# Gram products for two samples at a time in every tile, with two turning banks instead of four

## The reference

```python
e = jnp.stack([tbl_0[ids[:, 0]], ..., tbl_31[ids[:, 31]]], axis=1)
dots = jnp.einsum('bnd,bmd->bnm', e, e)
z = dots[:, iu, ju]                       # 496 pairs i < j
h = jnp.concatenate([z, dense_ctx], axis=1)
h = jnp.maximum(h @ W_top1 + b_top1, 0.0) # 512 -> 512
h = jnp.maximum(h @ W_top2 + b_top2, 0.0) # 512 -> 256
y = h @ W_top3                            # 256 -> 1
```

## Time and profile before

| | |
|---|---|
| median of 3 runs | 896.95 us (895.36 to 898.39) |
| profiled execution, its own time | 892.55 us |
| its span, first to last instruction | 890.7 us |
| TensorE matmuls | 601.0 us busy, 67%, 11019 matmuls |
| TensorE weight loads | 524.1 us, 59% |
| VectorE | 225.9 us, 25% |
| ScalarE | 204.6 us, 23% |
| GpSimd | 398.0 us, 45% |
| mean granted TensorE clock | 0.85 |

### The profile page before, as it was taken

How to read it: one execution, slowest core, us unless ns; L and a number is a source line. 1 busy time by engine, 2 the same in 40 slices (tenths; PEclk the granted TensorE clock), 3 DMA queues, 4 the chain that set the end, 5 groups by cost and what they waited for, 6 DMA issues and landing times.

```text
span 890.7 us, 24184 instructions
## 1 busy us (share of the span) xinstructions
PE 601.0 (67%) x11019; PEld 524.1 (59%) x11019; DVE 225.9 (25%) x578; ACT 204.6 (23%) x369; POOL 398.0 (45%) x426
## 2 busy tenths in 40 slices
PE   3557668486684867748577584875848668486687
PEld 2456557375572756737467474765737657375586
DVE  3444313123130231402223032231312313123122
ACT  4252303103030030401313022130210303103042
POOL 7563625526255361543715347262462625526220
PEclk9688969698796987969789697896969969698799
DMA  9962312313122141321313224131231312313110
GB/s 220 243 204 68 99 42 77 94 44 102 43 78 83 50 107 38 83 73 56 108 37 87 63 57 118 32 96 49 70 105 39 101 41 76 88 41 90 43 38 2
DMA packets 37459, 70.97 MB, mean 80 GB/s; under 512 B 10382, under 2 KB 23438, under 8 KB 37358
## 3 DMA queue, kind: packets, MB, share of 16 engines
q0 software_dynamic: 20112, 54.95, 22.1%
q1 hardware_dynamic: 17246, 14.48, 7.0%
HBM read 69.39 MB, written 0.01 MB: 78 GB/s over the span
## 4 chain that ended last, share of the span: by engine, by line
PE 42%; another core or an unknown queue 30%; issue 13%; ACT 12%; DMA 1%; DVE 1%; POOL 1%; ACTq 0%; DVEq 0%
PE look_ps L338 18%; PE quad_ps L358 12%; PE top_ps L420 6%; ACT turned L501 4%; ACT turned L483 3%; PE turn_ps L322 3%; PE quad_ps L322 2%; ACT area L550 2%; ACT ahead L490 1%; DMA rows<-in_tbl,row_ids 1%; PE quad_ps L377 1%; POOL rows L295 1%; PE top_ps L407 1%; ACT products L506 0%
## 5 line engine op out<-in xcount | busy, mean ns | idle before, releaser
L295 POOL DMA_INDIRECT rows<-in_tbl,row_ids x419 | 397.2, 948 | 458.1 <-PE turn_ps L322 184.1
L338 PE MATMUL look_ps<-one_hot,small 125*128 125x256 f32 (+1 forms) x1536 | 251.9, 303 | 104.7 <-issue 92.8
L338 PEld LDWEIGHTS look_ps<-one_hot,small 125*128 125x128 f32 x1536 | 214.0, 202 | 116.6 <-issue 112.3
L358 PE MATMUL quad_ps<-turned 128*32 128x31 f32 x7680 | 140.0, 204 | 121.8 <-issue 121.5
L358 PEld LDWEIGHTS quad_ps<-turned 128*32 128x32 f32 x7680 | 108.8, 115 | 166.9 <-issue 153.3
L674 DVE TENSOR_SCALAR one_hot<-ids_across,sub_row 125x256 fp32r<-125x256 int32 (+1 forms) x384 | 112.0, 364 | 145.8 <-PE look_ps L338 126.6
L322 PE MATMUL turn_ps<-ident,rows 128*128 128x128 f32 x424 | 64.5, 282 | 28.5 <-issue 14.7
L655 DVE TENSOR_TENSOR top_ps<-top_ps,b_sb 128x256 f32<-128x256 f32 x15 | 6.5, 433 | 299.8 <-PE top_ps L420 299.8
L490 ACT ACTIVATE ahead<-look_ps 128x512 f32<-128x512 f32 (+1 forms) x48 | 28.3, 590 | 232.5 <-PE look_ps L338 219.1
L407 PE MATMUL top_ps<-area,w_sb 128*128 128x128 f32 x488 | 61.9, 276 | 19.5 <-issue 18.8
L550 ACT ACTIVATE area<-top_ps,b_sb 128x128 f32<-128x128 f32 x61 | 17.5, 368 | 227.5 <-remote 225.2
(11 more groups left out here) (50 smaller groups left out, 169.9 us busy)
## 6 DMA issues: line engine op xcount, KB each, us to landing
rows<-in_tbl,row_ids POOLq DMA_INDIRECT x419
ids_across<-in_small_ids SPq DMA_DIRECT2D x45, 128.0 KB
landed<-in_tbl SPq DMA_DIRECT2D x6, 896.0 KB
w_sb<-in_W_top SPq DMA_DIRECT2D x4, 256.0 KB
landed<-in_tbl SPq DMA_DIRECT2D x6, 104.0 KB
w_sb<-in_W_top SPq DMA_DIRECT2D x1, 512.0 KB
area<-in_dense_ctx SPq DMA_DIRECT2D x16, 8.0 KB
row_ids<-in_ids SPq DMA_DIRECT2D x1, 240.0 KB
```

The lines of the kernel that those rows point to most:

```text
L295: pool.indirect_dma_start(out=rows[:, n % PLACES, j, :], out_offset=None, in_=tables[f], in_offset=bass.IndirectOffsetOnAxis(ap=row_ids[:, ...
L338: last = pe.matmul(look_ps[:, c * width:(c + 1) * width], small[:, f, r, part, c * P:(c + 1) * P], one_hot[n % 2][:, r, 0:width], start=(r ...
L358: last = pe.matmul(gram_ps[q * FIELDS:(q + 1) * FIELDS, g // BANK_GROUPS, at:at + COLS], turned[:, c, s, :], turned[:, c, s, 0:COLS], star ...
```

## The change

The scheme of the last tile is used in all tiles. `last_gram`, `last_unfold` and their semaphores go; `gram`, `unfold` and `align` take their place. The results take four banks of their own, so turning has two (`RING = 2`). Two units instead of four are turned early, after portions 5 and 6, and ScalarE's units are the even ones. ScalarE aligns banks 0 and 2, VectorE banks 1 and 3, in every tile. The ids of each tile are laid out on the host as those of the last tile were, so that neighbouring samples stand side by side.

```diff
-    ACT_UNITS = [0, 1, 2, 6, 8, 10, 12]
-    RING = 4
+    ACT_UNITS = [0, 2, 4, 6, 8, 10, 12]
+    RING = 2
-    EARLY_AFTER = [3, 4, 5, 6]
+    EARLY_AFTER = [5, 6]
-    BANK_GROUPS = GROUPS // 2
+    GRAM_BANKS = 4
+    BANK_GROUPS = GROUPS // GRAM_BANKS
-        quad_ps = psum("quad_ps", [P, LAST_BANKS, 512])
-        gram_ps = quad_ps[:, 0:2, :]
-        turn_ps = [psum(f"turn_ps{i}", [P, 512]) for i in range(RING - 2)] + [quad_ps[:, b, :] for b in (2, 3)]
+        gram_ps = psum("gram_ps", [P, GRAM_BANKS, 512])
+        turn_ps = [psum(f"turn_ps{i}", [P, 512]) for i in range(RING)]
...
                 for g in range(portion * GPP, (portion + 1) * GPP):
-                    at = g % BANK_GROUPS * COLS
-                    for c in range(CHUNKS):
-                        for q in range(QUADS):
-                            s = q * FIELDS + g
-                            last = pe.matmul(gram_ps[q * FIELDS:(q + 1) * FIELDS, g // BANK_GROUPS, at:at + COLS],
-                                             turned[:, c, s, :], turned[:, c, s, 0:COLS],
-                                             start=(c == 0), stop=(c == CHUNKS - 1))
-                if portion == PARTS - 1:
-                    last.then_inc(gram_done, 1)
+                    at = g % BANK_GROUPS * WIDE
                     for c in range(CHUNKS):
                         for h in range(HALVES):
                             s = QUADS * g + 2 * h
                             pair = turned[:, c, s:s + 2, :]
+                            last = pe.matmul(gram_ps[h * 2 * FIELDS:(h + 1) * 2 * FIELDS, g // BANK_GROUPS, at:at + WIDE],
+                                             pair.rearrange("d s f -> d (s f)"), pair[:, :, 0:COLS],
+                                             start=(c == 0), stop=(c == CHUNKS - 1))
+                if (portion + 1) * GPP % BANK_GROUPS == 0:
+                    last.then_inc(gram_banks, 1)
...
-                    for i in ACT_UNITS[:3]:
+                    for i in ACT_UNITS[:2]:
                         keep_turned(BEGIN[t] + i)
                     if FIRST[t] > FIRST[t - 1]:
                         keep_looked_up(FIRST[t] - 1)
+                    keep_turned(BEGIN[t] + ACT_UNITS[2])
                     pick(t - 1)
...
+                align(t, 0)
                 for n in range(FIRST[t], FIRST[t + 1] - 1):
                     keep_looked_up(n)
-            align(0)
-            align(2)
+                align(t, 2)
...
             def unfold(t):
-                dve.wait_ge(gram_done, t + 1)
+                dve.wait_ge(act_aligned, 4 * (t + 1))
+                dve.wait_ge(dve_aligned, 4 * (t + 1))
...
                 for k, n in enumerate(range(FIRST[t] + 1, FIRST[t + 1] + 1)):
+                    if n == FIRST[t + 1]:
+                        align(t, 1)
                     if n < len(LOOKUPS):
                         make_one_hot(n)
...
-            align(1)
-            align(3)
-            last_unfold()
+                    align(t, 1)
+                align(t, 3)
+            unfold(TILES - 1)
...
-    by_slot[-P:] = by_slot[-P:].reshape(P // FIELDS, FIELDS, -1).transpose(1, 0, 2).reshape(P, -1)
+    by_slot = by_slot.reshape(TILES, P // FIELDS, FIELDS, -1).transpose(0, 2, 1, 3).reshape(BATCH, -1)
```

More of the change, by code:

```diff
@@ L81, in dlrm_tower @@
     GPP = GROUPS // PARTS
-    BANK_GROUPS = GROUPS // 2
     HALVES = 2
     WIDE = 2 * COLS
-    LAST_BANKS = 4
-    LAST_GROUPS = GROUPS // LAST_BANKS
+    GRAM_BANKS = 4
+    BANK_GROUPS = GROUPS // GRAM_BANKS
     AT_ONCE = 2
@@ L157, in dlrm_tower @@
         last_h1 = [top_ps, look_ps, turn_ps[0], turn_ps[1]]
-        last_h2 = turn_ps[2]
+        last_h2 = gram_ps[:, 0, :]
         spare_ps = turn_ps[0]
@@ L166, in dlrm_tower @@
         high_ps = [bank[0:SP, 0:AT_ONCE * D].rearrange("p (r d) -> p r d", r=AT_ONCE)
-                   for bank in (gram_ps[:, 1, :], top_ps)]
+                   for bank in (gram_ps[:, GRAM_BANKS - 1, :], top_ps)]
         square = products[:, 0:COLS * ZROW].rearrange("p (i j) -> p i j", j=ZROW)
@@ L191, in dlrm_tower @@
         dve_kept = sem("dve_kept")
-        gram_done = sem("gram_done")
-        last_gram_done = sem("last_gram_done")
+        gram_banks = sem("gram_banks")
         act_aligned = sem("act_aligned")
@@ L350, in gram @@
                         pe.wait_ge(unfolded, t)
-                if t == 0 and portion == PARTS // 2:
+                if t == 0 and portion * GPP == GROUPS - BANK_GROUPS:
                     pe.wait_ge(low_parts, SMALL * STEPS)
                 for g in range(portion * GPP, (portion + 1) * GPP):
-                    at = g % BANK_GROUPS * COLS
-                    for c in range(CHUNKS):
-                        for q in range(QUADS):
-                            s = q * FIELDS + g
-                            last = pe.matmul(gram_ps[q * FIELDS:(q + 1) * FIELDS, g // BANK_GROUPS, at:at + COLS],
-                                             turned[:, c, s, :], turned[:, c, s, 0:COLS],
-                                             start=(c == 0), stop=(c == CHUNKS - 1))
-                if portion == PARTS - 1:
-                    last.then_inc(gram_done, 1)
[L364 to L372, removed]
+                    at = g % BANK_GROUPS * WIDE
                     for c in range(CHUNKS):
@@ L456, in _ @@
                     look_between(t, k)
[L457 to L460, removed]
+                    gram(t, k)
                     if t > 0 and k == 0:
@@ L480, in keep_turned @@
                 if t > 0:
-                    act.wait_ge(gram_done, t)
+                    act.wait_ge(gram_banks, GRAM_BANKS * t)
                 f = unit[0]
@@ L514, in pick, with align @@
                 act.activation(features[:, CYCLIC:PAIRS], diagonal[:, 0:HALF, HALF], ACT.Copy).then_inc(picked, 1)
-            def align(b):
-                act.wait_ge(last_gram_done, b + 1)
-                both = quad_ps[:, b, 0:LAST_GROUPS * WIDE].rearrange("p (g h j) -> p h g j", h=2, j=COLS)
+            def align(t, b):
+                act.wait_ge(gram_banks, GRAM_BANKS * t + b + 1)
+                both = gram_ps[:, b, 0:BANK_GROUPS * WIDE].rearrange("p (g h j) -> p h g j", h=2, j=COLS)
                 for q in (1, 3):
@@ L606, in keep_turned @@
                 if t > 0:
-                    dve.wait_ge(gram_done, t)
+                    dve.wait_ge(gram_banks, GRAM_BANKS * t)
                 f = unit[0]
@@ L613, in unfold, with align @@
             def unfold(t):
-                dve.wait_ge(gram_done, t + 1)
+                dve.wait_ge(act_aligned, 4 * (t + 1))
+                dve.wait_ge(dve_aligned, 4 * (t + 1))
                 if t > 0:
                     dve.wait_ge(picked, t * PICKS)
[L617 to L623, removed]
+                grams = gram_ps[:, :, 0:BANK_GROUPS * WIDE].rearrange("p b (g h j) -> p h j b g", h=2, j=COLS)
+                dve.transpose(square[:, 0:COLS, 0:FIELDS], grams[:, 0, :, :, :]).then_inc(unfolded, 1)
+            def align(t, b):
+                dve.wait_ge(gram_banks, GRAM_BANKS * t + b + 1)
+                both = gram_ps[:, b, 0:BANK_GROUPS * WIDE].rearrange("p (g h j) -> p h g j", h=2, j=COLS)
                 for q in (1, 3):
@@ L626, in align @@
                     dve.tensor_copy(both[at, 0, :, :], both[at, 1, :, :]).then_inc(dve_aligned, 1)
[L628 to L633, removed]
             def last_pick():
```

## The result

The changed kernel takes 945.76 us (median of 4 runs, 942.7 to 947.63), the kernel before beside it 896.15 us (4 runs, 894.34 to 898.39): 1.0549 times as long, with an interval of 1.0506 to 1.0592. Forecast were 927 us, and 885 to 960 as the range. The profiled execution's own time is 943.9 us, its span 942.1. Medians are of all executions of a kernel and ratios of its fast ones alone, those within 1.5% of its fastest; the two part company only for `after_paced2`, of whose ten executions five count (median 892.80 us, 900.99 of all ten).

What follows compares the result with a forecast made beforehand. Gathers in flight, not TensorE's work, were taken to bound the creeping stretch. Terms 5.0 - 5.0 + 1.8 + 0.2 - 0.85 + 0.8 = +1.95 us a period, x 14 = +27, ends +5.5, gave 927 us, range 885 to 960.

Steps and rivals of the forecast that it cites:

- the ends: First gram stage -3.5 us, prologue +3 (0 to 8), last turning stage +6; together +5.5 us.
- A longer burst, priced by gathers: Turning stage: 22 gathers back to back, four more at 1.251 us; stretch ends 4.1 us after the last, +5.0 us a period.
- GpSimd's queue was not to run dry: During the burst: a unit feeds GpSimd for 2.5 us and units are turned faster than that.
- Early holes hidden: Gram stage: two of four disturbed portions remain, their holes covered by 43 matmuls handed over, under 55; -5.0 us a period.
- The late last signal: End of the gram stage: 0.6 us a period taken within the early-holes term, bounds 0 and 2.8.
- The products: Gram portions: 32 wider matmuls at 30 ns, 0.95 us against 0.70 for 64; +1.8 us in seven portions a period.
- A cost by the number of matmuls: Rival on gram portions: 11 ns a product whatever its columns, 0.35 us a portion; about 860 us, chance 0.02.
- Left over from the burst: Behind the creeping stretch: +0.5 us for work left over, +0.3 for low clock, +0.2 for the first portion.
- Two banks: Turning at 0.75 us a unit puts layer 1 about 6 us later, costing nothing while gathers run.
- The hold did not end sooner: Rival at the burst's end: TensorE free 1.5 us after the last gather, not 4.1; about 881 us, chance 0.17.
- Turning did not become the bound: Rival in the creeping stretch: transpositions 1.46 us apart outlast the burst, starved gathers easing it; 983 us, chance 0.10.
- Loss and gain did not cancel: Rival over the whole period: nothing left over, second hole hidden, +0.55 us a period; about 901 us, chance 0.05.

Runs made afterwards that it cites:

- after_paced2: Changed kernel with two small scratch-block writes by GpSimd after each unit's gathers, from the second tile on: 892.80 us, 0.9981 times the kernel before.
- early2_b: Kernel before with two units turned early (after portions 5 and 6) instead of four, four turning banks kept: 931.21 us, 1.0402 times the kernel before.
- after_again: Second profile of the unaltered changed kernel; layer 1 comes 10.7 us after the 15th unfold, and what follows that unfold takes 37.6 us.
- the third group: Runs of early2_b, early2_ring2_b and after_paced2, beside the kernel before at 895.07 us.
- The pair without gathers: Kernel before and changed kernel, each with gathers of the first tile alone: 532.67 and 651.5 us, one execution each.
- after_paced: Changed kernel with four small scratch-block writes by GpSimd after each unit's gathers, from the second tile on: 708.79 us, 0.7914 times the kernel before.
- before_paced: Kernel before with four small scratch-block writes by GpSimd after each unit's gathers, from the second tile on: 779.72 us, 0.8706 times the kernel before.
- early2_ring2_b: Kernel before with two early units, two turning banks and even ScalarE units, products still four-wide: 938.66 us, 1.0476 times the kernel before.
- the second, third and fourth groups: Follow-up runs: gathers spaced out; parts of the change and half the pause; banks with pauses. Kernel before: 895.95, 895.07 and 563.58 us.

## Why the prediction was right, and where its sizes were off

In sum: forecast were +30 us and measured are +50. Of the 19 us that are missing in the profiled span, 17 are 14 periods at 1.2 us too little and 2 are the ends. The direction rests on the mechanism and not on luck; the size was wrong by over a third of the loss, and in the product's price, the late signal and the leftover every error went the same way. The forecast's own range of 903 to 950 also doesn't come out of the bounds named behind it: leftover of 0 to 2.5 us for 0.8 and prologue of 0 to 8 for 3 give some 913 to 956.

*A longer burst, priced by gathers: right.* Forecast was a stretch of some 32.5 us after the end of the stage, the last gather plus 4.1. Measured are 32.65 and 4.57 us. The same stands in `early2_b`. That gathers hold TensorE is shown by the spacing, with TensorE's instructions untouched. It isn't the whole cause: in the free surroundings the same bursts hold nothing. The prediction had no word for that, nor had its profile.

One step of this term was wrong, at no cost: GpSimd's queue was not to run dry. In five of the 14 periods of this profile it does (in none of `after_again`). In the first fence below, of the period whose unfold is at 268.01, the gather before 293.75 was at 290.08: the unit whose turn lets it go had been turned by 284.86 and was seen late. The second fence is of the shortest period, 55.8 us.

```profile
293.75 0.94 POOL L291 DMA_INDIRECT rows<-in_tbl,row_ids  x1 [2.72 <-remote]
...
297.50 0.95 POOL L291 DMA_INDIRECT rows<-in_tbl,row_ids  x1 [0.31 <-issue]
...
300.00 0.80 PE L334 MATMUL look_ps<-one_hot,small 125*128 125x256 f32 x3 [0.61 <-issue]
```

```profile
703.64 0.94 POOL L291 DMA_INDIRECT rows<-in_tbl,row_ids  x1 [3.49 <-remote]
703.81 2.48 PE L334 MATMUL look_ps<-one_hot,small 125*128 125x256 f32 x10
```

In the first the last gather comes 29.5 us after the unfold and not 27.1, but TensorE goes on at much the same point, 32.0 us and not 31.7: 2.5 us after that gather and not 4.6. In the second, with 4.4 us from one gather to the next, TensorE goes on in one go although two more gathers follow. Taken to TensorE's last idle time ahead of layer 2, the wait behind unbroken bursts was 4.0 to 4.2 us in every period of the kernel before and 3.0 to 4.8 us after 22 gathers. So the prediction's "last gather plus 4.1" is no rule. A hold that adds up while gathers come fast and is worked off in a pause fits these rows, and the third group too.

*Early holes hidden: right.* The portions at 436.03 and 439.01 have none, and so it is in all 14 periods. Ahead of a hole in `early2_b` go 10 look-ups and 45 products; in the changed kernel it is 11 and 32, which fit. The Trainium skill ("TensorE: Matmul & The Clock Gate", the table ahead of its first section) has a queue of 64; the 55 here are a little less, as the earlier trace rows had them.

*The late last signal: mis-sized.* I took 0.6 us; TensorE was through at 440.09, VectorE began at 441.34: 1.25. In the kernel before it is 0.11 (475.94 to 476.05), so the change adds 1.15.

*The products: mis-sized.* 1.08 us a portion (425.55 to 426.63) and not 0.95. The 30 ns of the earlier trace rows came from seven portions in one go, and I had no row for 32 products between look-ups. The seven portions after the first take 7.6 us in all and took 10.7, holes and one portion of 0.85 us included: -3.1, where 1.8 - 5.6 = -3.8 was forecast. A cost by the number of matmuls is out: 34 ns each, against 11.

*Left over from the burst, +1.0 in the forecast (0.2, 0.5 and 0.3): some +1.3.* Seven look-ups and the whole first portion stand behind the stretch, the latter for 1.98 us, and L399 starts 3.7 us after its end. L399 itself is faster, which gives part back.

The period shown lasts 58.24 us (383.10 to 441.34), 1.7 over my 56.5: 0.1 for the stretch, 0.3 left over, 0.55 for the signal and 0.75 for the portions. Periods differ, from 55.8 to 58.4 us, with a mean of 57.7; so a period came to +3.16 us on the mean and not +1.95. The term that was off most is the price of a product.

*Two banks: right while gathers run, not shown at the ends.* Nothing while gathers run, and +2.7 us in the prologue (forecast +3, one profile each). In the changed kernel, whose first stage has early gains too, the first unfold hardly moved (forecast -0.5). What follows the 15th grew by 7.1 us in one pair of profiles and by 1.8 in the other (forecast +6), and it can't be put down to the banks: from the unfold to layer 1 the last tile takes 11.6 or 10.7 us in the changed kernel and 6.0 or 7.2 in the kernel before, but 10.7 in `early2_b` too, which keeps four banks. There two more units are left to turn, and TensorE waits 1.25 us for the last one's rows.

*The rivals.* The hold did not end sooner: 4.57 us after the last gather, not 1.5. Turning did not become the bound: layer 1 started 11.4 us before the last gather. It came 15.7 us after the unfold, though, where I had some 12, and in the two periods with 3.6 us between two gathers of the burst it came after 21 us. What that rival said would ease it, starved gathers, is what happened there. Loss and gain did not cancel.

*What stays open.* What makes the surroundings hold or free: the chip, or something that changes on one chip with time. Whether the hold acts on TensorE's queue or on the semaphores: both look late at once, and no run parts them. What of a gather does it, its issue by GpSimd or its transfer: spacing changes both, and only the last 2 us of the tail stand without transfers. The pair without gathers ran in the free surroundings alone. Whether the pair products alone hide the holes between spaced gathers: `after_paced` has none and `before_paced` has them, but the two also differ in banks and early units. What products and aligns cost apart from the rest where TensorE is held: the changed kernel's 1.0526 and 1.0549 and `early2_ring2_b`'s 1.0476 have intervals that overlap.

## What to carry to other kernels

Where TensorE has many short idle times put down to "issue" or to an unknown queue, set them against the indirect gathers on GpSimd's queue before counting TensorE's work; if they end some microseconds after each unbroken burst's last gather (3.0 to 4.8 here), the burst is what is paid for, and spacing it out can win more than the rearrangement did (0.87 alone and 0.79 with it, against 1.05). Fewer, larger matmuls bought nothing by themselves: an undisturbed portion went from 0.69 to 1.08 us. What they can hide is the holes beside gathers, and only where there are such holes. Price them from a row that has them between the same neighbours. And time a version of this kind beside the old one at more than one place and time: the same pause takes 13% off the kernel before in the holding surroundings and adds 12% to its variant with two banks in the free ones.

## What the runs showed of the hardware

- Whether gathers hold TensorE differs between groups of runs, and a chip number doesn't settle it (the second, third and fourth groups carry number 11): 892 to 898 us against 560 to 567 us for the same kernel. The gathers follow each other at 1.25 us in both.
- Where they do, the hold has a point below which it builds up: units of two gathers every 3.2 us leave no creeping stretch (`before_paced`, `after_paced`; the first keeps short holes), every 2.7 us they do (`after_paced2`).
- It outlasts the transfers: TensorE goes on 3.0 to 4.8 us after the last gather of an unbroken burst, and creeps from 414 to 415 while the DMA engines move nothing. Where two gathers of the burst stood 3.6 us apart, it went on 2.5 us after the last.
- Signals come late in it. The turn that started at 398.94 had ended at 400.02, and ScalarE, idle, took it up at 408.75.
- Without gathers 64 products of 32 by 31 columns take 0.69 us and 32 of 64 by 62 take 1.08, 11 ns and 34 ns each.
